# Long convolution, norm and ternary feed-forward: two of five staging slots loaded from the sync queue, 32 casts a tile instead of 40

## The reference

```python
# every channel is convolved along the sequence with a filter of 2048 taps
conv = irfft(rfft(xT, n=pad) * rfft(filt[::-1], n=pad), n=pad)[..., L-1:L-1+seq]
x = layernorm(x + conv)
h = silu(x @ w1.T * s1) * (x @ w2.T * s2)      # 1024 -> 4096
h = gelu(h @ h1.T * sh1)                       # 4096 -> 4096
h = gelu(h @ h2.T * sh2)                       # 4096 -> 4096
x = layernorm(x + h @ w3.T * s3)               # 4096 -> 1024
```

## Time and profile before

| | |
|---|---|
| median of 3 runs | 4127.0 us (3960.89, 4127.0, 4277.67) |
| profiled execution, its own time | 3965.67 us |
| its span on the slowest core | 3964.1 us (cores 3928.1 to 3964.1) |
| TensorE busy / VectorE / ACT / POOL | 72% / 18% / 8% / 12% |
| DMA | 709 MB, 179 GB/s |

### The profile page before, as it was taken

One profiled execution on the slowest core, in us unless ns is written; L12 is line 12 of the kernel. 1 busy time (PEld: TensorE's weight loads), 2 busy tenths in 40 slices (PEclk: granted clock), 3 DMA queues, 4 the chain that ended last, 5 costly groups with the idle time before them and its releaser, 6 DMA issues.

```text
span 3964.1 us, 39367 instructions; the slowest of 8 cores (3928.1 to 3964.1 us)
## 1 busy us (share of the span) xinstructions
PE 2839.3 (72%) x13920; PEld 1371.5 (35%) x13920; DVE 723.4 (18%) x1397; ACT 297.4 (8%) x461; POOL 490.4 (12%) x890
## 2 busy tenths in 40 slices
PE   0442233242340777999969999969999996999995
PEld 0211111111110333444624444454444463444445
DVE  4333333433433120000041000032000004100003
ACT  0000000000000110000011001002100101101000
POOL 2233333343333010000000000000000000000000
PEclk9866667666675888999989999989999998999998
DMA  5788878888788575333534333444344443443332
GB/s 162 204 217 219 252 223 257 234 253 263 228 256 237 160 245 172 149 149 149 173 125 159 149 149 149 156 142 174 134 156 153 158 154 130 159 159 154 149 149 96
DMA packets 321267, 709.02 MB, mean 179 GB/s; under 512 B 72800, under 2 KB 236704, under 8 KB 294448
## 3 DMA queue, kind: packets, MB, share of 16 engines
q1 hardware_dynamic: 93440, 398.50, 27.8%
q0 software_dynamic: 80176, 207.28, 18.8%
q10 hardware_dynamic: 147456, 100.73, 8.5%
HBM read 588.91 MB, written 113.25 MB: 177 GB/s over the span
## 4 chain that ended last, share of the span: by engine, by line
PE 60%; DMA 21%; DVE 7%; issue 4%; POOL 3%; DVEq 2%; ACTq 2%; ACT 1%; SPq 0%; POOLq 0%
PE ps L166 57%; DMA wstgf<-h 10%; DMA wstgf<-w 4%; DMA h2s<-wstgb 3%; PE ps L164 3%; POOL x1bf L365 2%; DMA w3s<-wstgb 2%; DVEq L60 2%; DVE wstgb L238 1%; ACTq L252 1%; DMA xstg<-x 1%; DVE stats L292 1%; POOL wstgf L233 1%; DVE sqs L293 1%; DVE sqs L295 1%
## 5 line engine op out<-in xcount | busy, mean ns | idle before, releaser
L166 PE MATMUL ps<-gT,hsl 128*128 128x512 bf16 x3968 | 883.7, 381 | 48.0 <-ACT uT L471 43.5
L166 PE MATMUL ps<-uT,hsl 128*128 128x512 bf16 x3968 | 877.3, 379 | 4.3 <-ACT uT L471 4.3
L166 PE MATMUL ps<-xwh,Fh 128*128 128x512 bf16 x544 | 226.8, 417 | 791.4 <-DVE xwl L279 791.4
L166 PE MATMUL ps<-x1T,wsl 128*128 128x512 bf16 x1792 | 436.2, 384 | 236.7 <-DMA wsl<-w2s 137.9
L166 PEld LDWEIGHTS ps<-gT,hsl 128*128 128x128 bf16 x3968 | 389.3, 98 | 522.7 <-issue 59.8
L166 PEld LDWEIGHTS ps<-uT,hsl 128*128 128x128 bf16 x3968 | 388.0, 98 | 473.4 <-issue 6.2
L238 DVE CAST wstgb<-wstgf 128x512 bf16<-128x512 f32 x704 | 303.1, 431 | 705.6 <-DMA wstgf<-h 375.7
L529 DVE TENSOR_TENSOR y<-ps,s3bt 128x256 f32<-128x256 f32 x64 | 27.2, 425 | 1940.9 <-PE ps L164 1940.9
L166 PEld LDWEIGHTS ps<-xwh,Fh 128*128 128x128 bf16 x544 | 57.6, 106 | 873.4 <-issue 821.2
L233 POOL DMA_DIRECT2D wstgf<-h x512 | 287.9, 565 | 385.4 <-DVE wstgb L238 315.6
L166 PEld LDWEIGHTS ps<-x1T,wsl 128*128 128x128 bf16 x1792 | 176.9, 99 | 453.9 <-issue 248.1
(11 more groups left out here) (52 smaller groups left out, 711.9 us busy)
## 6 DMA issues: line engine op xcount, KB each, us to landing
wstgf<-h POOLq DMA_DIRECT2D x512, 256.0 KB, 5.4
hsl<-h1s SPq DMA_DIRECT2D x64, 2048.0 KB, 8.6
hsl<-h2s SPq DMA_DIRECT2D x64, 2048.0 KB, 8.5
wstgf<-w POOLq DMA_DIRECT2D x192, 256.0 KB, 6.2
h2s<-wstgb ACTq DMA_DIRECT2D x512, 64.0 KB, 4.4
wsl<-w1s SPq DMA_DIRECT2D x32, 1024.0 KB, 6.5
wsl<-w2s SPq DMA_DIRECT2D x32, 1024.0 KB, 7.9
hsl<-w3s SPq DMA_DIRECT2D x16, 2048.0 KB, 8.9
```

The source lines that it names most:

```text
L166: sc.run("tensor", lambda t, a=lt, b=rh, o=out_ap, s=st: t.matmul(o, a, b, start=s, stop=False))
```

## The change

The filter's pieces use slots 0 to 2 alone. The load of a cast job goes to SP's queue where its slot is 3 or 4, and stays on POOL's for slots 0 to 2. Each tile emits 32 casts instead of 40, so that 17 + 512 = 529 jobs lie before the feed-forward part and 175 in the h1 stage of quarter 0.

```diff
     for c in range(WIN):
-        sl = c % 5
+        sl = c % 3
...
             sl = i % 5
-            sc.waits("gpsimd", wstgf_slot[sl].r)
-            e_l = sc.run("gpsimd", lambda g, srch=srch, ic=ic, c0=c0, w=w, sl=sl:
+            lq = "gpsimd" if sl < 3 else "sync"
+            sc.waits(lq, wstgf_slot[sl].r)
+            e_l = sc.run(lq, lambda g, srch=srch, ic=ic, c0=c0, w=w, sl=sl:
                          g.dma_start(wstgf[sl][:, 0:w], srch[ic * 128:(ic + 1) * 128, c0:c0 + w]), inc=s_wld[sl], k=16)
...
-        emit_casts(40)
+        emit_casts(32)
```

## The result

| | before | changed |
|---|---|---|
| median of 10 runs | 4095.2 us (3946.8 to 4277.7) | 4384.8 us (4366.4 to 4744.2) |
| profiled execution, own time | 3965.67 us | 4369.75 us |
| span on the slowest core | 3964.1 us | 4368.2 us |

The changed kernel takes 1.105 times as long (95% interval 1.102 to 1.109).

What follows compares the result with a forecast made beforehand. The prediction took TensorE (60% of the chain) and DMA (21%) as bounds, with engines 0.95 busy during casts. 3965.7 + 12 + 246 + 45 - 160 + 253 = 4362, plus 40 for run spread: 4400 us, range 4180 to 4700.

Steps and rivals of the forecast that it cites:

- The 40 us on top of the sum: Whole kernel: a quarter of the 161 us by which the profiled execution lies under the median of the runs.
- filter and first chunks: Convolution's start: three slots slow 14 filter pieces, +5 us; three early casts' loads queue behind stores on SP, +7.5; together +12.
- casts of h1 in the tiles: Convolution, 256 casts: loads on SP wait behind stores, 2.25 us a cast instead of 1.29, +246 us (bounds +177, +433).
- casts of w1, w2 in the tiles: Convolution, 111 casts: three of ten wait for a load issued late, 2.0 us each, +45 us (bounds -3, +133).
- 128 casts less, of h2: Convolution's h2 tiles: nothing blocks SP, pace stays 1.25 us, and each cast moved out takes its 1.25 along, -160 us.
- h1 stage: Feed-forward part: eleven groups, each block's hsl issued behind late cast loads on SP, 41.4 us each, +253 us (bounds +183, +344).
- The order in SP's queue: H1 tiles: loads of slots 3 and 4 stand behind stores of casts 2 and 3, so neither is issued ahead.
- the landing: H1 tiles: time from a load's issue to its data, taken as 3.5 us, between 2.9 and 5.4; two per five casts.
- rival 1: Tiles: SP's queue hides the blocked loads, pace stays 1.29 and 1.59 us; 4071 us, 2.6% slower; chance 0.05.
- rival 4: Whole kernel: nothing measurable, tile casts keep their pace and the h1 stage takes its cheap end; 4001 us; chance 0.03.
- Rival 2: Feed-forward h1 blocks: hsl isn't late, each group costs 15.9 us, +127 instead of +253; 4236 us, 7% slower; chance 0.08.
- The rival of the other sign: All 512 tile casts: two queues shorten landings to 2.9 us, 0.78 us a cast; 3782 us, 4.6% faster; chance 0.04.

Runs made afterwards that it cites:

- experiment 4: The changed kernel with the stores of w1, w2 and h1 all on ACT's queue, so SP has loads alone during the convolution: ratio 1.023 to the kernel before.
- experiment 5: The changed kernel, same queues, but in the convolution the store of job i is emitted after the load of job i + 3: ratio 1.033.
- experiment 3: The changed kernel with each h1 block's hsl load issued ahead of the block's casts: 4287.0 us at the fastest, ratio 1.091 to the kernel before.
- experiment 1: The kernel before with 32 casts a tile instead of 40, all loads still on POOL's queue: ratio 0.990.
- 7: The kernel before with 32 casts a tile, hsl ahead of the casts, and feed-forward cast stores on SP's queue instead of ACT's: ratio 0.990.
- experiment 10: The kernel before with 32 casts a tile, hsl ahead, feed-forward cast loads and stores on POOL's queue, stores three jobs late: ratio 0.956.
- experiment 8: As 7, with tiles' h2 stores alternating SP and ACT, hsl early in h2 too, 6 casts per h1 block, 5 per h2 block: ratio 0.953.
- experiment 9: As experiment 8, with 28 casts a tile, 8 in each block of h1 and 7 in each of h2: ratio 0.950.

## Why the prediction was right

It said 4400 us, range 4180 to 4700, and slower with 0.92. The median is 4384.8; the sum against the profiled execution was 4362 and this execution took 4369.75. Such a close sum has errors that cancelled, the tiles and the start 46 us too low and the h1 stage 38 too high. The 40 us on top of the sum came from the spread of the runs and not from a row; the median lies 23 over the sum, and that 4400 is so close is in part luck. Each term:

| term | said | measured | from |
|---|---|---|---|
| filter and first chunks | +12 | +19 | end of the 17th chunk at 136.2 and 117.2 us |
| casts of h1 in the tiles | +246 | +279 | 256 x ((96.5 - 20.3) / 32 - 1.29) |
| casts of w1, w2 in the tiles | +45 | +51 | tiles of 85.9 us, 2.05 a cast |
| 128 casts less, of h2 | -160 | -160 | h2 tiles of 60.9 for 70.9 us, 1.25 each |
| h1 stage | +253 | +215 | 487 and 272.5 us |
| the rest | 0 | 0 | 2258 us, equal on both sides |

*The order in SP's queue* was right in mechanism and pattern, and experiments 4 and 5 show it as the cause. Mis-sized was the landing, the one term for which no row stood. I took 3.5 us for these loads, because fewer are in flight. SP's 90 loads in the seven h1 tiles land after 4.0 us in the middle (2.6 to 6.8), against 5.4 before. In the chain above they are 4.54, the second of a pair, and 5.24, the first of the next; the first is the longer one, as said. These two and 3.7 us for the rest make the 13.5 us from 720.06 to 733.56, 2.7 a cast. With 4.0 the sum 4.1 + 2 x 4.0 gives 2.42 a cast, and the tiles' average is 2.38. The announced DMA share of 0.6 came as 0.55. By this pace rivals 1 and 4, which kept 1.29, are out. The 6.9 us that the prediction took for ten w casts beside their landings stand in no row; its 2.0 a cast came as 2.05.

*Start.* The filter pieces cost 6.4 us in place of 5 (the first chunk's copy begins at 29.97 and not 23.58). The 17 chunks lost another 12.6 instead of 7.5. VectorE's waits for cast loads grew by 8.0 us (1.8 to 9.8), nearly as said. Its waits for the chunks' own loads grew by 4.9 (46.1 to 51.0), which I had at nothing: on ACT a chunk's load stands behind the store of a cast, and comes as late as that cast.

*The h1 stage* has eleven waits ended by `hsl`, as said, of 22 us instead of some 25. From the end of one group's block to the end of the next it is 38.0 us on average, where I said 41.4. The casts before the issue of `hsl` took 9.8 us in the block shown (1663.3 to 1673.0) where I said 11, the landing 12.0 in the middle where I said 13. (The casts of the earlier trace rows are the tenth and eleventh of their group, not the ninth and tenth.) Rival 2, that `hsl` is not late, was wrong; with `hsl` early (experiment 3) the stage is 71 us shorter.

*One step of the reasoning fell.* I read the 23.8 us of ACT's stores as what holds a block, and priced a group at 47.7 / 3 = 15.9 us by it. No row gives the 47.7: the rows give 271.4 - 221 = 50.4, 16.8 a group. Either price came near in experiment 1, where eleven groups cost 170 us over the 221 of the blocks, 15.5 each (the stage at 391 us, where 271 + 127 = 398 was said). But the same casts tied to SP instead (7) cost about the same (404 us), and tied to nothing (10) cost TensorE nothing. What cost was that a block may not begin before its 16 casts are through, at the pace of the casts while the DMA engines are 0.9 busy.

*The Trainium skill's rule* that several issuing queues share the same 16 engines ("DMA: Bandwidth & Descriptors", "Issuing engines are not separate DMA queues") agrees with the runs: with the order mended (experiment 4) loads on two queues give h1 tiles of 61.8 us on average, and on one (experiment 1) 60.4. The second queue brought nothing. The rival of the other sign is out by this too: with two queues the loads land after 5.2 and 5.3 us, with one after 5.3, and the pace stays at 1.30 us a cast, well above 0.98.

**A version that beats both.** Experiments 8 and 9, 0.953 and 0.950 of the kernel before: loads on POOL alone, `hsl` ahead of the casts in SP's order, late stores on SP, late casts spread thinly over the blocks. Experiment 10 gets as far (0.956) with one queue given over to the casts.

## What to carry to other kernels

Before a DMA issue is moved to another queue, write down that queue's list in program order around its new place: a prefetch behind a store that waits for the work just done is no prefetch any more, and a weight load behind someone else's loads inherits all their waits. Background work that was moved to a stage with free bandwidth cost the foreground nothing where no step of it stood behind that work in any queue (experiment 10), and the whole of its own pace where one did (1 and 7). When an experiment takes a wait from one queue and an equal one shows up in another, it has not yet told a full resource from an order; untie the work from every queue of the foreground, and see.

## What was not expected of the hardware

With the DMA engines 0.85 busy at 295 to 299 GB/s, TensorE ran 440 us of 512-column matmuls at a granted clock of 1.00 with one wait of 1.07 us, for a GELU (experiment 10). And landings shorten by only a quarter when the engines are half idle: 4.0 us in the middle for a load of 256 KB on SP's queue and 4.9 on POOL's at a share of 0.55, against 5.4 on POOL's in the h1 tiles of the kernel before, where the casts hold the share at 0.95.
